# Expert tiles: a step's four 64x64 remainder products between the even and the odd tile's main down products

## The reference

```python
scores = jax.nn.softmax(t @ gate_w.T, axis=-1)
weights, indices = jax.lax.top_k(scores, TOP_K)          # 2 of 16 experts
for e in range(N_EXPERTS):
    w_e = jnp.sum(jnp.where(indices == e, weights, 0.0), axis=-1)
    y = y + _swiglu(t, w1[e], w3[e], w2[e]) * w_e[:, None]
z = _swiglu(t, sw1, sw3, sw2)                            # shared experts, width 352
```

## Time and profile before

| | |
|---|---|
| Median of three executions | 674.37 us (673.14 to 675.02) |
| The profiled execution's own time | 674.55 us |
| Its span, first to last instruction | 672.7 us |
| Granted TensorE clock, mean | 0.968 |
| TensorE products busy | 598.8 us, 89% |
| VectorE, ScalarE, GpSimd busy | 528.5, 536.5, 427.1 us |
| The expert pairs | about 508 to 635 us |

### The profile page before, as it was taken

The page is one execution under the profiler, slowest core; times in us unless marked ns, Lnnn a source line. Parts: engine busy times, 40 slices in busy tenths (PEclk is TensorE's granted clock), DMA queues, the critical chain, the costliest instruction groups (busy, mean ns, idle before and its releaser), DMA issues.

```text
span 672.7 us, 12802 instructions
## 1 busy us (share of the span) xinstructions
PE 598.8 (89%) x4478; PEld 490.4 (73%) x4479; DVE 528.5 (79%) x899; ACT 536.5 (80%) x1222; POOL 427.1 (63%) x261
## 2 busy tenths in 40 slices
PE   5798999999994789799999999899999787878983
PEld 3388999999993445699999999895775444434562
DVE  6798999999998799999999999886735654445364
ACT  2999999999995988999999999974537665454535
POOL 0028999999997103699999999960041565655402
PEclk8979999999997889999999999998999999999987
DMA  7012333333330000254544454381120222222163
GB/s 193 6 65 78 109 111 111 111 101 112 108 106 0 2 2 23 75 149 158 151 156 139 140 165 142 106 272 63 64 63 17 87 79 79 87 78 78 64 251 125
DMA packets 41596, 67.77 MB, mean 101 GB/s; under 512 B 6688, under 2 KB 20928, under 8 KB 41536
## 3 DMA queue, kind: packets, MB, share of 16 engines
q1 hardware_dynamic: 37696, 56.50, 26.8%
q0 software_dynamic: 3840, 10.49, 4.9%
HBM read 57.28 MB, written 9.70 MB: 100 GB/s over the span
## 4 chain that ended last, share of the span: by engine, by line
ACT 55%; PE 24%; DVE 12%; issue 3%; POOL 2%; DMA 2%; another core or an unknown queue 1%; DVEq 1%; ACTq 0%; POOLq 0%; SPq 0%
ACT rings L1046 26%; ACT rings L1034 10%; ACT late L1034 10%; PE both L1489 7%; PE both L1475 5%; PE bank L1501 3%; PE bank L1495 2%; DVE st L444 2%; ACT tok_a L924 1%; DVE rings L805 1%; ACT rings L924 1%; ACT tok_a L997 1%; POOL residual L1206 1%; ACT w_sb L989 1%
## 5 line engine op out<-in xcount | busy, mean ns | idle before, releaser
L1196 POOL TENSOR_TENSOR arena<-arena,rings 128x1024 f32<-128x1024 f32 x126 | 296.3, 2372 | 13.4 <-DVE arena L659 8.9
L1395 PE MATMUL both<-rings,tok_a 128*128 128x128 f32 x1152 | 171.7, 278 | 3.7 <-DVE arena L659 2.9
L1395 PEld LDWEIGHTS both<-rings,tok_a 128*128 128x128 f32 x1152 | 148.6, 191 | 7.8 <-ACT rings L1046 3.6
L659 DVE TENSOR_TENSOR_SCAN arena<-rings,both 128x1024 f32<-128x1024 f32 x64 | 143.8, 2275 | 9.5 <-ACT rings L1034 6.4
L659 DVE TENSOR_TENSOR_SCAN arena<-late,both 128x1024 f32<-128x1024 f32 x62 | 139.3, 2273 | 8.2 <-ACT late L1034 6.5
L1424 PE MATMUL bank<-ident,arena 128*128 128x128 f32 x1024 | 133.0, 273 | 3.5 <-POOL arena L1196 2.4
L1424 PEld LDWEIGHTS bank<-ident,arena 128*128 128x128 f32 x1024 | 115.6, 141 | 4.6 <-POOL arena L1196 2.7
L1046 ACT ACTIVATE rings<-tok_a,b_tok 128x256 f32<-128x256 f32 x224 | 101.5, 493 | 0.0
L1046 ACT ACTIVATE rings<-ident,b_tok 128x128 f32<-128x128 f32 x288 | 96.3, 386 | 0.3
L1397 PE MATMUL both<-ident,rings 128*128 128x128 f32 x448 | 90.7, 273 | 0.0
L1211 POOL TENSOR_TENSOR arena<-arena,feat_a 128x512 f32<-128x512 f32 x8 | 19.4, 2424 | 87.2 <-DVE arena L555 87.2
(11 more groups left out here) (238 smaller groups left out, 1072.5 us busy)
## 6 DMA issues: line engine op xcount, KB each, us to landing
rings<-c_rows SPq DMA_DIRECT2D x128, 256.0 KB, 3.3
w_sb<-w SPq DMA_DIRECT2D x18, 352.0 KB, 4.2
arena<-w SPq DMA_DIRECT2D x2, 2048.0 KB, 12.6
residual<-x SPq DMA_DIRECT2D x4, 512.0 KB, 5.7
x_rows<-tok_a SPq DMA_DIRECT2D x4, 512.0 KB, 2.6
tok_a<-y_tok SPq DMA_DIRECT2D x4, 512.0 KB, 6.7
w_sb<-y_tok SPq DMA_DIRECT2D x4, 512.0 KB, 7.5
out<-residual SPq DMA_DIRECT2D x8, 256.0 KB, 2.6
```

Source lines behind the costliest of these rows:

```text
L659: dve.tensor_tensor_scan(h_s, decay_s.rearrange("p h t -> p (h t)"), both[s % B_RING][:, :], 0.0, ALU.mult, ALU.add).then_inc(h_ready, 1)
L1196: pool.tensor_tensor(h_both, h_both, c_row, ALU.mult).then_inc(hc_ready, 1)
L1395: pe.matmul(o, tok_a[:, c, h * P:(h + 1) * P], v_ring[:, s % V_RING, j, 0:P], start=True, stop=True)
```

## The change

The even tile's main products come first, then the remainders of both tiles, then the odd tile's main products. The flags that start and close the sum of the odd tile's bank change places accordingly, and the odd tile's `ty_ready` is raised by its main products. The waits of both tiles stand ahead of the first product: a step waits for the turned rows, the staged weights and the staged remainder rows of both tiles.

```diff
             def down_main(e, k):
 
                 for t, w in zip(token_halves, (w2a[:, e, :], staged_down[:, k, 0])):
-                    pe.matmul(ysum[k][t, 0:D], gatedT[:, k, 0, t], w, start=True, stop=False)
+                    ins = pe.matmul(ysum[k][t, 0:D], gatedT[:, k, 0, t], w, start=k == 0, stop=k == 1)
+                return ins
 
             def down_rest(k):
 
                 r = token_halves[k]
                 for t, w in zip(token_halves, (staged_rest[r, :], staged_down[r, k, 1])):
-                    ins = pe.matmul(ysum[k][t, 0:D], gatedT[r, 0, 3, t], w, start=False, stop=True)
+                    ins = pe.matmul(ysum[k][t, 0:D], gatedT[r, 0, 3, t], w, start=k == 1, stop=k == 0)
                 return ins
...
                         pe.wait_ge(ty_copied, at(i - 1))
                     else:
                         pe.wait_ge(moe_copied, SHARED_FIRST)
-                    pe.wait_ge(tgT_copied, at(i + 1))
-                    pe.wait_ge(down_staged, at(i + 1))
-                    if i % 2:
-                        pe.wait_ge(rest_staged, at(i + 1))
-                    down_main(bass.ds(expert(i), 1), i % 2)
-                for i in (2 * j, 2 * j + 1):
-                    down_rest(i % 2).then_inc(ty_ready, 1)
+                for staged in (tgT_copied, down_staged, rest_staged):
+                    pe.wait_ge(staged, at(2 * j + 2))
+                down_main(bass.ds(expert(2 * j), 1), 0)
+                down_rest(0).then_inc(ty_ready, 1)
+                down_rest(1)
+                down_main(bass.ds(expert(2 * j + 1), 1), 1).then_inc(ty_ready, 1)
```

## The result

The changed kernel takes 684.41 us (median of five runs, 682.29 to 686.48) against 674.37 us before (672.79 to 676.89): ratio 1.0137, 95% interval 1.0109 to 1.0165. It is slower by 10.0 us by the medians, 9.2 us by the ratio; the forecast was 669.1 us.

The account below looks back on a forecast made before the run. It took a closed ring of 6.46 us per held step (scatter to second gather 3.87, to VectorE's copy 1.88, to next scatter 0.71) as the bound; 674.55 - 6.4 + 1.0 gave 669.1 us, range 666.5 to 677.5.

Parts of the forecast that it names:

- What an early signal gives a held step: Steps with late TensorE signals: an earlier even-tile signal and scatter save 0.43 us in each of 15 steps, 6.4 us.
- Then the first case returns: Held steps alternate between signal early (6.21 us) and signal held (5.84 us); two take 12.05 instead of 12.90.
- the hold on the later signals: TensorE's transposes' signal, delayed while GpSimd's gather is under way, was taken as still released at about 563.2 us.
- GpSimd runs 0.8 us ahead of TensorE: After an early scatter: the next second gather comes at 566.85 us, the next signal 0.70 us behind it, held.
- The even tile's signal: TensorE's remainders signal to VectorE's copy moves from 0.52 to 0.09 us behind the second gather's issue, the change's whole chance.
- held all the same: Rival: the hold begins with or before the second gather, held steps keep 6.46 us; 675.5 us, chance 0.33.
- VectorE is busy: Rival: VectorE can't use the early signal at once; busy until 562.25 us, 0.86 us left, priced in the sum.
- no issue: TensorE's clock in the expert-pair steps: granted 1.00, the 2.4 GHz level, so no term for it.
- Hidden by the up products, with 0.15 us to spare: Even main's added wait for staged remainder rows in held steps: could start at 559.85, before 560.00 us, so no cost.
- The change of mode: TensorE's switch between 128-row and 64-row products: one more per step, 0.10 us, hidden in held steps, paid in free ones.
- The free steps: Steps at the loop's end without the hold: added waits and mode changes cost +1.0 us together, between +0.3 and +2.5.
- The slower rival: Rival: one more mode change on TensorE lengthens the hold; 677.0 us, up to 684.4 if staging shows, chance 0.22.

Follow-up runs that it names:

- e2: Changed kernel, but the even tile's ready signal is raised by the first of the odd tile's two last products; 676.46 us, 1.0006 of the kernel before.
- e9: Changed kernel, with GpSimd's even-tile scatter also waiting for the last signal TensorE gives in the step; ratio 1.0062 to the kernel before.
- e1: Kernel before, old product order, with all three waits for both tiles ahead of the even main products; 675.81 us, ratio 1.0007.
- e3: Kernel before without the 32 gathers behind the first eight; 656.77 us, ratio 0.9713.
- e7: Kernel before without its 32 later gathers and with all three waits ahead of the even main products; 662.07 us, ratio 0.9802.
- e4: Changed kernel without the 32 gathers behind the first eight; 666.47 us, ratio 0.9858 to the kernel before.
- e11: Kernel before with the scatters of tiles 8 to 39 moved behind the last tile; eight steps with two gathers each take 5.12 to 5.66 us.
- e6: Kernel before with products ordered main, remainders, main, remainders per pair and all three waits ahead of the first; ratio 1.0108.

## Why the prediction was wrong

**The step that failed** is "What an early signal gives a held step", in its sentence "The transposes' signal is still held until about 563.2, so L805 starts there", and what follows from it up to "Then the first case returns". It took the hold on the later signals as fixed, released as before, while it moved the scatter up. The scatter is part of what holds them. In place of 6.21 and 5.84 us in turn the changed kernel shows 6.81 and 7.62 in the pair above, and 13.96 to 14.82 us for each of its five such pairs in place of 12.05. e2 takes out the early signal, and with it the early scatter, and returns to 1.0006; e9 keeps the signal and puts the scatter back, and the 7.6 us steps go. By what means the scatter prolongs the hold is not shown. The same section named the danger ("GpSimd runs 0.8 us ahead of TensorE") and counted it as a gain.

**The even tile's signal.** Right that it can get past: 0.87 to 1.25 us behind the gather instead of 1.88, but in five of the fifteen steps only. In four "held all the same" came (1.85 to 1.94 us), and these cost no more than before. "VectorE is busy" cost nothing.

**The clock** was "no issue" in the kernel before. In the changed kernel one step of the fifteen ran at 0.76 of the full clock and lost some 1.7 us by it, which the sum has no term for. It isn't the cause: the other four pairs take 13.96 to 14.82 us at a full clock.

**The waits.** "Hidden by the up products, with 0.15 us to spare" held as long as nothing else moved (e1; e2's main at 2.41 us). In the changed kernel it doesn't hold, since held transposes make staging late: the main runs 4.28 us behind the up products. It is where the price is paid, not the cause.

**Products and free steps.** The change of mode stands at the 0.10 us forecast (554.50 to 554.82 between the last main and the first remainder, 0.22 of it spacing). The free steps were put at +0.10, +0.49 and +0.4, about 1.0 us together, and nothing for the last pair. They show +0.38, +0.43 and +0.69 (5.46, 5.71 and 5.16 us for 5.08, 5.28 and 4.47), 1.50 together, and the last pair +0.58. From the start of the last pair's step to the end of the kernel it is 41.0 us against 41.8, so 0.74 us is left of it: the total is near the forecast, its parts are not. Without gathers the whole loop shows the same term, +0.39 a step, half waits and half order (e3, e7, e4). The Trainium skill's page "TensorEngine Tiling (Array Packing)", section "Key Properties", has the drain at a change of mode; e2 pays it in every step, and its steps of 6.60 us are 0.02 us from the 6.58 of e1, which has the old order.

**The slower rival** gave up to 684.4 us, and 684.41 was measured, but by another mechanism (TensorE's own order lengthening the hold), which e2 refutes. Its chance of 0.22 was for the wrong reason, and the number is a coincidence. The rival that was missing, the scatter that closes its own pause, could be read from the earlier trace rows: the pause of 1.6 us ahead of the scatter is the only one in GpSimd's step, and the signals come in it.

## What to carry to other kernels

When a signal is late because of someone else's traffic, ask what the earlier signal will start, and whether that is more of the same traffic. A pause in a busy queue can be when the other engines' signals arrive: before closing it, list every signal that now arrives in it. And price a forecast's gain with the whole ring moved, not with one link moved and the release times of the others kept.

## What the runs showed of the hardware

I had not expected that the hold goes with how many of GpSimd's indirect DMAs follow each other rather than with what they do: two a step (0.30 us between DMAs) hold nothing that matters, be they scatters (e3, L827 0.77 us behind the remainders) or gathers (e11, L827 4.07 to 4.22 us behind the up products); in the kernel before four hold TensorE's completion signals by 1.36 us, until some 1.9 us behind the fourth; seven hold them by 4.4 and 5.2 us, in the one step that has them (e11). It is no rule yet. In e3 and e11 the two DMAs also stand elsewhere in the step, from about 4.7 us behind the up products on, so number and place aren't told apart, and in the first steps of e6 four in a row hold nothing that a waiting engine shows. Leaving the later gathers out, and the hold with them, took 19 us of 676 (e3). It shows as waits that end on "remote", and as several signals let go almost together. Which part of the chip holds them back the traces don't tell.
